# CoPE attention: the selection product in four row groups, its two halves around a 512-column product, and a new order of the steps

## The reference

```python
Q, K, V = heads(q, Wq_w, Wq_b), heads(k, Wk_w, Wk_b), heads(v, Wv_w, Wv_b)
logits = jnp.einsum('bhqd,bhkd->bhqk', Q, K) / jnp.sqrt(d)
gates = jax.nn.sigmoid(logits)
pos = jnp.flip(jnp.cumsum(jnp.flip(gates, -1), -1), -1)    # sum of the gates from this key on
pos = jnp.minimum(pos, 63)
logits_int = jnp.einsum('bhqd,dn->bhqn', Q, pos_emb)       # 64 positions
cope = (jnp.take_along_axis(logits_int, ceil(pos), -1) * w
        + jnp.take_along_axis(logits_int, floor(pos), -1) * (1 - w))    # w = pos - floor(pos)
out = jnp.einsum('bhqk,bhkd->bhqd', jax.nn.softmax(logits + cope, -1), V)
```

## Time and profile before

| | us |
|---|---|
| median of 3 runs | 14988.53 (14980.4 to 15003.98) |
| the profiled execution: its own time | 14944.12 |
| its span, first to last instruction | 14942.4 |
| of it, `build_cope_attention` (4211 to 14193 us) | 9982 |
| busy in the span: PE / PEld / DVE / ACT / POOL | 12056.5 / 8114.4 / 7374.0 / 4440.9 / 6514.9 |

### The profile page before, as it was taken

How to read it: one execution, slowest core, us unless ns; L and a number is a source line. 1 busy time by engine, 2 the same in 40 slices (tenths; PEclk the granted TensorE clock), 3 DMA queues, 4 the chain that set the end, 5 groups by cost and what they waited for, 6 DMA issues and landing times. The chain is left out here.

```text
span 14942.4 us, 176465 instructions
## 1 busy us (share of the span) xinstructions
PE 12056.5 (81%) x56950; PEld 8114.4 (54%) x56950; DVE 7374.0 (49%) x13140; ACT 4440.9 (30%) x7890; POOL 6514.9 (44%) x5384
## 2 busy tenths in 40 slices
PE   8787888887668888888888888888888888888745
PEld 3553222223446666666666666666666666666622
DVE  0112333332236666666666666666666666666533
ACT  0111222221123333333333333333333333333310
POOL 0000000000036666666666666666666666666500
PEclk9888777777778888888888888888888888888766
DMA  3112222222123333333333333333333333333223
GB/s 75 52 44 52 54 54 52 51 54 60 64 68 78 79 80 83 83 80 80 80 78 82 83 81 79 80 80 80 83 83 80 80 81 80 80 83 83 62 72 102
DMA packets 1062473, 1096.94 MB, mean 73 GB/s; under 512 B 746498, under 2 KB 853762, under 8 KB 996882
## 3 DMA queue, kind: packets, MB, share of 16 engines
q1 hardware_dynamic: 988690, 1087.84, 30.3%
q10 hardware_dynamic: 73728, 8.42, 0.4%
HBM read 884.93 MB, written 210.76 MB: 73 GB/s over the span
## 5 line engine op out<-in xcount | busy, mean ns | idle before, releaser
L921 PE MATMUL c_pickps<-c_table,c_hot 128*128 128x112 f32 x16384 | 3468.2, 388 | 564.6 <-DVE c_over L1212 541.7
L921 PEld LDWEIGHTS c_pickps<-c_table,c_hot 128*128 128x128 f32 x16384 | 3299.6, 266 | 669.5 <-DVE c_over L1212 568.2
L1302 POOL TENSOR_TENSOR c_total<-c_total,c_over 128x384 f32<-128x384 f32 (+3 forms) x3584 | 3289.3, 918 | 465.3 <-DVE c_over L1212 185.7
L1302 POOL TENSOR_TENSOR c_total<-c_total,c_middle 128x1024 f32<-128x1024 f32 x512 | 1210.0, 2363 | 2854.6 <-DVE c_middle L1203 2854.6
L1189 DVE COPY_PREDICATED c_pickps<-c_upper,c_pickps 128x256 f32<-128x256 uint32 (+1 forms) x1024 | 799.0, 826 | 3352.2 <-PE c_pickps L921 3352.2
L1269 POOL IOTA c_digitrow<- 1x128 f32 x1 | 0.3, 255 | 4210.8 <-POOLq L65 4210.8
L1054 ACT ACTIVATE c_over<-c_place,c_thresholds 128x384 f32<-128x384 f32 (+3 forms) x3584 | 1589.3, 525 | 0.0
L1212 DVE TENSOR_TENSOR c_over<-c_over,c_pickps 128x384 f32<-128x384 f32 (+3 forms) x3584 | 1407.1, 452 | 0.0
L1037 ACT ACTIVATE c_place<-c_gateps 128x512 f32<-128x512 f32 x1024 | 611.4, 597 | 2674.4 <-PE c_gateps L894 2674.3
L894 PE MATMUL c_gateps<-c_qa,c_ka 128*128 128x512 f32 x2048 | 1105.2, 622 | 65.8 <-ACT c_place L1037 65.1
L960 PEld LDWEIGHTS c_softps<-c_v,c_probs 128*128 128x128 f32 x8192 | 1062.3, 208 | 138.2 <-issue 104.7
(11 more groups left out here) (213 smaller groups left out, 13740.9 us busy)
## 6 DMA issues: line engine op xcount, KB each, us to landing
c_hot<-t_digits SPq DMA_DIRECT2D x512, 1024.0 KB
t_tables<-c_tablesb SPq DMA_DIRECT2D x256, 256.0 KB, 5.6
c_table<-t_tables SPq DMA_DIRECT2D x1024, 56.0 KB, 2.3
a_q<-t_qa SPq DMA_DIRECT2D x384, 128.0 KB, 2.7
a_k<-t_ka SPq DMA_DIRECT2D x384, 128.0 KB, 3.1
c_kb<-t_kb SPq DMA_DIRECT2D x256, 128.0 KB, 6.2
t_digits<-c_anchorrows SPq DMA_DIRECT2D x128, 256.0 KB, 2.4
c_ka<-t_kb SPq DMA_DIRECT2D x128, 128.0 KB, 5.5
```

What stands on the lines that cost most here:

```text
L921: mm = nc.tensor.matmul(pick_ps[:, h // 4, 0:WIDTH, r * 8:(r + 1) * 8], hot[t % 2][:, h, :], table[s][:, :, :, t * 16 + h].rearrange("p l ...
L1302: nc.gpsimd.tensor_tensor(a, a, b, ALU.add).then_inc(s_add, 1)
```

## The change

1. **Selection in row groups.** Each 128x128 by 112-column product becomes four of 32 rows by 28 columns: row group g takes partitions 32g to 32g+31 of `hot` and the two lanes of the table that lie there, and writes to bank g. Calls go from 16 to 64 a tile. `keep_table` and the anchor's layout follow: the anchor is no longer permuted by DVE (line 1169), and `table_sb` is permuted by ACT in runs of 16.
2. **Two halves.** `pick` runs 8 of its 16 groups h, then one product of another kind (a gate product in slots 0 and 1, `turn_anchor` in slot 2, the second table product in slot 3), then the other 8.
3. **Order.** `logits` of tile n-1 move to the head of slot n, `values` of tile n-2 stand between them and `add_cope`. On DVE `top` and `top_row` move behind some products, `less` and `compare` behind all of them, and `compare` works two tiles ahead. `near` moves behind `less`.
4. **Rounding chain.** `near` keeps its third intermediate in `rounded` (SBUF), not in `gate_ps` (PSUM); `turn_anchor` waits only for the anchor and that step, not for all six.
5. **SP.** The load of V moves behind the load of `hot` for tile 3.

```diff
             def turn_anchor(i):
-                pe.wait_ge(s_near, i + 1)
                 pe.wait_ge(s_anchor, i + 1)
+                pe.wait_ge(s_edge, 4 * i + 6)
...
-            def pick(i, s, t, turn=None):
+            def pick(i, s, t, between):
...
                 for h in range(16):
-                    if h == 8 and turn is not None:
-                        turn_anchor(turn)
-                    r = h % 4
-                    mm = nc.tensor.matmul(pick_ps[:, h // 4, 0:WIDTH, r * 8:(r + 1) * 8], hot[t % 2][:, h, :],
-                                          table[s][:, :, :, t * 16 + h].rearrange("p l m -> p m l"), start=True, stop=True)
+                    if h == 8:
+                        between()
+                    for g in range(4):
+                        rows, lanes = slice(32 * g, 32 * g + 32), slice(2 * g, 2 * g + 2)
+                        mm = nc.tensor.matmul(pick_ps[:, g, 0:WIDTH, h:32:16], hot[t % 2][rows, h, :],
+                                              table[s][rows, lanes, :, t * 16 + h].rearrange("p l m -> p m l"),
+                                              start=True, stop=True)
...
-                nc.scalar.activation(table_sb[n][:, :].rearrange("p (l x) -> p l x", l=8), gate_ps[:, :].rearrange("p (x l) -> p l x", l=8),
-                                     ACT.Copy).then_inc(s_tablesb, 1)
+                nc.scalar.activation(table_sb[n][:, :].rearrange("p (l t h) -> p l t h", l=8, t=4),
+                                     gate_ps[:, :].rearrange("p (t l h) -> p l t h", t=4, l=8), ACT.Copy).then_inc(s_tablesb, 1)
...
-                nc.vector.tensor_scalar(anchor[:, :].rearrange("p (t l h) -> p t h l", t=4, l=8),
-                                        rounded[:, :].rearrange("p (t h l) -> p t h l", t=4, l=8), EIGHTS, None, ALU.subtract).then_inc(s_anchor, 1)
-                nc.vector.scalar_tensor_tensor(out=gate_ps[:, :], in0=rounded[:, :], scalar=EIGHTS, in1=gate_ps[:, :],
+                nc.vector.tensor_scalar(anchor[:, :], rounded[:, :], EIGHTS, None, ALU.subtract).then_inc(s_anchor, 1)
+                dve.wait_ge(s_anchor, i + 1)
+                nc.vector.scalar_tensor_tensor(out=rounded[:, :], in0=rounded[:, :], scalar=EIGHTS, in1=gate_ps[:, :],
                                                op0=ALU.subtract, op1=ALU.subtract).then_inc(s_edge, 1)
...
                     mux(i, s, t)
-                    if behind:
+                    for k in range(2):
+                        product(i, s, t, k)
+                    if two:
+                        recip(n - 2, x)
+                    product(i, s, t, 2)
+                    if one:
                         top(n - 1, 1 - x)
...
+                    if t == 3 and ahead:
+                        compare(4 * i + 4, 0, 2 * i + 3)
+                    if one:
+                        less(n - 1, 1 - x)
+                    if t < 2:
+                        compare(n + 2, x, 2 * i + 2)
+                    elif t == 2 and ahead:
                         near(i + 1, 1 - s)
-                    if behind:
-                        recip(n - 1, 1 - x)
+                    elif t == 3 and ahead:
+                        compare(4 * i + 5, 1, 2 * i + 3)
```

More of the change, by code:

```diff
@@ L845, in step @@
                 load_hot(i, s, 3)
+                if not final(i):
+                    load_v(i + 1, 1 - s)
                 if not final(i, 2):
@@ L858, in _ @@
             load_b(0, 0)
+            load_v(0, 0)
             send_tables(0, 0)
@@ L962, in values, with piece @@
                 mm.then_inc(s_pv, 1)
[L964 to L970 removed]
+            def piece(i, t, at):
+                if t < 2 and at < 4 and not final(i):
+                    gates(i + 1, 4 * t + at)
+                elif t == 3 and at in (0, 3) and not final(i, 2):
+                    tables(i + 2, at // 3)
@@ L972, in step @@
             def step(i, s):
+                ahead = not final(i)
                 for t in range(4):
                     n, x = 4 * i + t, t % 2
-                    behind = not (isinstance(n, int) and n == 0)
-                    ahead = not final(i)
-                    if behind:
+                    one = not (isinstance(n, int) and n < 1)
+                    two = not (isinstance(n, int) and n < 2)
+                    if one:
+                        if t:
+                            logits(i, s, t - 1)
+                        else:
+                            logits(i - 1, 1 - s, 3)
+                    piece(i, t, 0)
+                    if two:
+                        if t < 2:
+                            values(n - 2, x, 1 - s)
+                        elif t == 2:
+                            values(n - 2, x, s, i)
+                        else:
+                            values(n - 2, x, s)
+                    if one:
@@ L978, in step @@
                         add_cope(n - 1, 1 - x)
-                    if ahead:
-                        pieces(i, t, 0)
-                    if behind:
                         turn_peak(n - 1, 1 - x)
-                    if ahead:
-                        pieces(i, t, 1)
-                    if behind:
+                    piece(i, t, 1)
+                    if one:
                         bases(n - 1, 1 - x)
-                    if ahead:
-                        pieces(i, t, 2)
-                        if t == 2:
-                            places(i + 1, 1 - s)
@@ L991, in step @@
-                    logits(i, s, t)
-                    if ahead:
-                        pieces(i, t, 3)
-                    if behind:
-                        if t == 0:
-                            values(n - 1, 1 - x, 1 - s)
-                        elif t == 1:
-                            values(n - 1, 1 - x, s, i)
-                        else:
-                            values(n - 1, 1 - x, s)
-                    if ahead:
-                        pieces(i, t, 4)
+                    piece(i, t, 2)
@@ L1003, in step, with between @@
+                    if t == 2 and ahead:
+                        places(i + 1, 1 - s)
+                    def between():
+                        if t == 2 and ahead:
+                            turn_anchor(i + 1)
+                        piece(i, t, 3)
                     if t < 3:
-                        pick(i, s, t + 1, i + 1 if t == 2 and ahead else None)
+                        pick(i, s, t + 1, between)
                     elif ahead:
-                        pick(i + 1, 1 - s, 0)
@@ L1007, in step @@
-                    if ahead:
-                        pieces(i, t, 5)
+                        pick(i + 1, 1 - s, 0, between)
             for n in range(2):
@@ L1017, in _ @@
                 tables(1, n)
-            pick(0, 0, 0)
+            pick(0, 0, 0, lambda: None)
             quads(pe, step)
+            logits(last, 1, 3)
+            values(4 * last + 2, 0, 1)
             add_cope(4 * last + 3, 1)
@@ L1104, in step @@
                         past(i + 1, 1 - s, 0)
-                    if t == 2 and ahead:
-                        keep_anchor(i + 1)
-                    if behind:
-                        if t:
-                            norm(i, s, t - 1)
-                        else:
-                            norm(i - 1, 1 - s, 3)
+                    if t < 2 and ahead:
+                        lift(i + 1, 1 - s, t)
             for n in range(2):
@@ L1123, in _ @@
             quads(act, step)
+            norm(last, 1, 2)
             keep_base(4 * last + 3, 1)
```

68 lines of the change are left out of this document (30 added, 38 removed).

## The result

The changed kernel takes 16109.31 us (median, 16086.6 to 16127.97) against 14984.47 (14968.79 to 15003.98): ratio 1.0749, 95% interval 1.0729 to 1.0769. It is 7.5% slower, where 2.6% faster was predicted. Its profiled execution took 16086.6 us, with a span of 16084.9.

The account below looks back on a forecast made before the run. DVE and `pick` in turn were taken as the bound, with a DMA path beside them. 42.5 + 16.1 + 15.2 = 73.8 us a quad against 77.0, over 127 quads less one-time costs, saved 393 us: 14595 us, range 14400 to 14800.

Parts of the forecast that it names:

- The pick in row groups: `pick` as 32 rounds of four overlapping loads: 5.0 us a tile, against 6.3 to 6.8 before.
- Rival C: In `pick`, loads overlap but the four column streams don't: 6.1 us, 76.4 us a quad, 14920 us; chance 0.14.
- D: Pairs in `pick` follow no faster than at line 932: 7.1 us, 78.8 us a quad, 15230 us; chance 0.18.
- 12.1 + P: Length of slots 0 and 1: 12.1 us of other work and waits, plus `pick`, giving 17.1 us.
- P: Time of one tile's `pick` in row groups, forecast at 5.0 us.
- A to M1: From the end of `turn_anchor` to tile 1's `mux`: set by DMA, 42.5 us instead of 42.4.
- slot 1: From tile 1's `mux` to tile 2's: 16.1 us instead of 17.6, TensorE having run ahead by 1.0.
- M2 to A: From tile 2's `mux` to the end of `turn_anchor`: 15.2 us instead of 17.1.
- Rival B: TensorE at the full clock throughout: `pick` 3.5 us, 69.7 us a quad, 14080 us; chance 0.13.
- A to M0: From the end of `turn_anchor` to tile 0's `mux`: 24.4 us, set by the second `hot` load and `compare`.
- Slot 0: From tile 0's `mux` to tile 1's: bound by DMA (third `hot` load), staying near 18 us.

Follow-up runs that it names:

- e12: Kernel of e1 with each selection product as four calls of 32 rows, each with all 112 columns: 15442.38 us, ratio 1.0323.
- e1: Changed kernel with the wide selection product of before (128 rows, 112 columns) and its layouts, still in halves: 14694.24 us, ratio 0.9839.
- e4: Kernel before with the rounding chain alone (third step to SBUF, anchor's transposition waiting for fewer steps): 14833.45 us, ratio 0.9917.
- e11: Kernel of e1 with `pick` not cut in halves in three of four slots: 14844.43 us, ratio 0.9933.

## Why the prediction was wrong

**The pick in row groups: right.** Halves of 1.99 us at full clock and 3.63 at half. Their mean is 2.63, so `pick` takes 5.3 us, with 5.0 forecast. That the two come so close is in part luck: both levels were priced low (3.5 and 6.6 us for what takes 4.0 and 7.3). Rivals C and D are out: the four groups overlap, and 64 pairs in 1.99 us are 0.031 us each, against line 932's 0.055. Of the two rules of the Trainium skill that I weighed, 62 ns a matmul where firmware decodes it (TensorE: Matmul & The Clock Gate, Wait — 56ns, not 53.3ns?) is twice what these took, so it did not bind here. The slowing by outputs without neighbours (PSUM — Partial Sum Buffer, Specifications) can't have cost more than is in those 0.031 us; no run changes the output's layout alone, so its size isn't shown.

**The sum for a slot, "12.1 + P": wrong, and this is the step that failed.** I took the share of the slow clock from the trace of before, and applied it to P alone. The 12.1, a row of TensorE's other work, was priced at the full clock: 1.2, 1.0, 2.0 and 1.9 us for `logits`, a gate product, `values` and `add_cope`, which end 5.8 us after `mux`. They take 2.06, 2.08, 3.46 and 3.76 us at half clock and end 10.5 after it; in the mean of all quads `add_cope` ends 11.7, 7.4, 6.1 and 10.5 us after the `mux` of slots 0 to 3. The new order had put just this row in front of DVE's `top`. And the share itself was taken as given, where the change to the pick moved it: slots 0 to 3 had 1.00, 0.90, 0.75 and 0.84 and now 0.74, 1.00, 0.72 and 0.50 in the quads shown, and 0.69, 0.84, 0.74 and 0.53 in the mean. The sum came out so: A to M1 51.0 us against 42.5, slot 1 17.8 against 16.1, M2 to A 16.9 against 15.2, together 85.8 against 73.8. Rival B names the clock, but upwards, and its argument against (shorter picks leave TensorE idle longer) isn't what happened: TensorE is as busy as before. No rival had the clock falling.

**A to M0: wrong by the same step.** Forecast A + 24.4, set by the second load. In the quad shown `pick` of tile 0 starts at A + 19.8 instead of 16.3, since slot 3's products, and `compare` behind them, came late behind `add_cope`. Its halves with the table product take 9.2 us, and `mux` follows at A + 29.2, set by TensorE; the second load's `compare` ends at A + 26.9. **Slot 0:** I had DMA as its bound; in the quad shown the next `mux` waits 2.03 us for `pick`. **Slot 1:** 17.8 us in the mean against 16.1, so wrong; with the full clock, as in the quad shown, it is 15.1 and the sum is a microsecond too high. **M2 to A:** 16.9 in the mean against 15.2, with a tenth of the quads at 13.6 or less. In the quad shown `turn_anchor` starts 15.8 us into slot 2 instead of 13.1, by `places` as I had named it: its two products end at 12.6 instead of 10.2, since `values` and `add_cope` ahead of it and `places` itself ran in part at half clock.

**The program's length: not in the prediction.** I counted the pick's instructions as time on TensorE, not as bytes. Its turn costs some 150 us here, and 465 in e12.

**What the change without its first part is worth: underestimated.** Rival C, with a pick of 6.1 us, has 76.4 us a quad and 14920 us, 68 us gained. e1, with 6.6, took 75.2 a quad and gained 256. The row beside the pick was priced too long for the full clock: slot 1 of e1, at 0.99 of it, is 17.1 us, 10.6 beside a pick of 6.5, where the sum has 12.1. Of the 256 e4 gives 117; the other 139 need the halves, as e11 shows.

**Where the expected gain went.** e1 less the changed kernel is 1415 us. Returning the columns alone (e12) gave back 667 us, although it made every pick longer and left the long program in; these I put down to the clock. Of the 748 between e12 and e1, 465 stand at the loop's turn in e12, a pause and the lower clock behind it. How the remaining 280 or so divide isn't separated. In the changed kernel itself the turn shows as 150 only, because slot 0 is slow without it, so the shares don't simply add. Why a weight load with few columns behind it goes with a lower clock isn't shown, only that it did at any height and number tried.

## What to carry to other kernels

Before making a TensorE step shorter, price everything else on TensorE at half clock, above all what stands in series with another engine: the step's form can take the clock from its neighbours. Look at the granted clock as soon as a rewrite puts fewer columns behind each weight load: here it was 0.83 or more with 112, 0.74 with 56 and 0.58 to 0.72 with 28. Many small products that overlap well can be fast by themselves and slow for the kernel. Count a loop body's instructions when a rewrite multiplies them, and look at the bytes of the instruction queue.
